# Two cross-attention stages: which PSUM bank holds what, and in which order TensorE, ScalarE and VectorE use them

## The chip, the cores and the metric
One core of a Trainium2 chip runs the whole program. The metric is device time in microseconds: the median of three executions.

## The reference, cut to what matters
Six residual stages on x (2 sequences of 256 tokens, width 256), each on the layer-normed x. The first and the fourth are cross-attention to a context of 4096 rows of width 256:

```python
q = (x @ Wq); k = (context @ Wk); v = (context @ Wv)      # stage 1: 8 heads of 64; stage 4: 16 heads of 16, with biases
scores = einsum("bhnd,bhmd->bhnm", q, k) * scale
out = einsum("bhnm,bhmd->bhnd", softmax(scores), v)
x = x + out @ Wo + bo
```

The others are local and latent attention, a dense mixture of experts, a linear recurrence, and a mixture over sorted chunks. They are not touched.

## The kernel before, in words
Each cross-attention runs over four units (a sequence and half of the heads), and a unit over eight chunks of 512 context rows: 32 chunks. A chunk of the context is loaded into `c_in` (SyncE), transposed on TensorE (`turn`, two banks of four 128x128 transposes, line 935), and split into a high part `c_hi` (ScalarE, `context_high`, line 641) and a low part `c_lo` (VectorE, `context_low`, line 1542), since matmuls take fp32r. From these come the keys (`keys`, in the first stage two tiles of six 512-column matmuls, in the fourth one, line 948) and values (`values`, two blocks of twelve 256-column matmuls each; in the fourth stage only for units 0 and 2). Keys are again split into a high part (lines 678, 679, 762) and a low part (`low_keys`, lines 1578, 1579, 1687).

Softmax needs the maximum over all keys before the first exponential. So for each chunk `maxima` multiplies high parts of keys and queries (lines 993 and 1148; two 512-column matmuls for each h, 8 matmuls a chunk in stage 1 and 16 in stage 4), and VectorE reduces each bank of 128x512 to one column (`reduce`, lines 1567 and 1676). Only when a unit's eight chunks are through does `shift_row` bring the negated maxima (DMA) into the row that the exact scores add. Scores, exponentials and mixtures therefore run LAG = 9 chunks behind: step t handles keys and values of chunk t, maxima of chunk t-1, and scores and mixtures of chunk g = t-9. Steps 1 to 8 have maxima only, steps 9 to 31 have all ("full steps"), the last ones scores and mixtures only. The program lists steps per engine by hand: every engine executes its instructions in the written order, with waits on semaphores between them.

PSUM has eight banks. Two pairs are `score[0]` and `score[1]` (1024 columns each), `bank[1]` gathers the mixture, and the other three are a `ring`: the uses of a step (denominators, maxima, keys, values, transposes) take the three in turn, and `freed0`/`freed1` say which earlier use's semaphore (`red`, `kl`, `v`, `cl`, `dc`) has to be waited for. In the fourth stage the order on TensorE in a full step is: score pair n and maxima pair n for n = 0 to 7, the first mixture after n = 5 (four heads, 32 matmul records of 256 columns, line 1161), keys, the second mixture, values, transposes of the next chunk. VectorE: all reductions, low part of keys, end of a unit (`finish`: reciprocal, product, bias), `context_low`, high queries (first step of a unit) and low queries (two in each of four steps). GpSimd copies the split keys into `st1` for the scores. Below, R, S and M are reductions, score pairs and maxima pairs.

## Time and profile before

| | us |
|---|---|
| median of 3 runs | 1932.55 (1932.42 to 1935.55) |
| the profiled execution | 1927.47 |
| its span, first to last instruction | 1925.5 |
| TensorE busy | 1664.0 |
| VectorE busy | 1117.2 |
| ScalarE busy | 793.3 |
| GpSimd busy | 499.8 |

A row of the timeline merges equal instructions that follow each other: start, length, engine, line, operation, output<-input, shapes, count, and in brackets the idle time before it with what ended it. PE is TensorE, PEld its weight loads, DVE VectorE, ACT ScalarE, POOL GpSimd. PEclk is the granted TensorE clock as a share of 2.4 GHz. Ends of matmuls are modelled, so starts are the safer reading.

### The profile page before, as it was taken

The page shows a single profiled execution, that of the slowest core. Times are in us where ns is not written, and L with a number is a line of the kernel's source. Part 1 is how long each engine was busy: PE and PEld are TensorE (multiplying, and loading weights), DVE is VectorE, ACT ScalarE, POOL GpSimd, SP SyncE. Part 2 cuts the span into 40 slices and gives each one's busy share as a digit, 9 for nine tenths or more (in the row PEclk, how much of TensorE's full clock was granted, in tenths as well). Part 3 has the DMA queues.
Part 4 walks back from the last instruction along what each step waited for, and adds up shares of the span by engine and source line. Part 5 has one row for each costly group of instructions (what it writes and reads, how often), then busy time and mean ns, then how long its engine had stood idle before and what let it go on. Part 6 is the DMA issues. An engine that isn't in the chain of part 4 may idle for free. (4 is left out here: it accounts for less than half of the span.)

```text
span 1925.5 us, 26912 instructions
## 1 busy us (share of the span) xinstructions
PE 1664.0 (86%) x10311; PEld 1208.0 (63%) x10311; DVE 1117.2 (58%) x1880; ACT 793.3 (41%) x1084; POOL 499.8 (26%) x630
## 2 busy tenths in 40 slices
PE   5889999999999668779997888999999899885289
PEld 3667777777777467568886555555566555342278
DVE  4766666666653465356654777776756777106651
ACT  3435554554544132224442111555556455661110
POOL 0003433433469000000000200443433434640000
PEclk9989999999999877679998777899999999997589
DMA  2112221222222100022230110111001010000243
GB/s 77 44 44 67 66 61 50 67 67 58 53 60 52 33 1 1 23 88 87 87 98 11 33 32 27 31 34 34 23 23 34 23 34 12 2 1 22 88 156 117
DMA packets 75443, 92.35 MB, mean 48 GB/s; under 512 B 7442, under 2 KB 62276, under 8 KB 75332
## 3 DMA queue, kind: packets, MB, share of 16 engines
q1 hardware_dynamic: 75140, 90.79, 15.8%
q8 instruction: 73, 1.20, 0.3%
q14 instruction: 38, 0.31, 0.1%
q10 hardware_dynamic: 192, 0.05, 0.0%
HBM read 73.47 MB, written 0.52 MB: 38 GB/s over the span
## 5 line engine op out<-in xcount | busy, mean ns | idle before, releaser
L571 POOL CAST st<-ef 32x512 fp32r<-32x512 f32 x384 | 233.0, 607 | 397.9 <-PE score L1136 354.4
L1676 DVE TENSOR_REDUCE mx<-bank 128x1 f32<-128x512 f32 x512 | 311.8, 679 | 42.2 <-PE bank L1148 41.6
L757 ACT ACTIVATE P<-score 128x1024 f32<-128x1024 f32 x256 | 255.9, 1025 | 129.1 <-PE score L1136 128.8
L1148 PE MATMUL bank<-ef,qm 128*128 128x512 f32 x512 | 234.4, 505 | 41.3 <-DVE mx L1676 21.4
L948 PE MATMUL bank<-c_hi,w_split 128*128 128x512 f32 x640 | 233.1, 425 | 23.7 <-DVE c_lo L1542 8.4
L1148 PEld LDWEIGHTS bank<-ef,qm 128*128 128x128 f32 x512 | 105.9, 207 | 154.9 <-DVE mx L1676 107.4
L1136 PE MATMUL score<-qs,st 97*128 97x512 f32 x512 | 173.3, 426 | 12.9 <-ACT P L757 8.7
L948 PEld LDWEIGHTS bank<-c_hi,w_split 128*128 128x128 f32 x640 | 128.7, 201 | 78.1 <-issue 39.8
L1567 DVE TENSOR_REDUCE mx<-bank 128x1 f32<-128x512 f32 x256 | 162.3, 682 | 22.1 <-PE bank L993 13.6
L536 POOL TENSOR_TENSOR sum<-sum,P 128x512 f32<-128x512 f32 x84 | 111.2, 1324 | 210.0 <-ACT P L673 210.0
L673 ACT ACTIVATE P<-score 128x1024 f32<-128x1024 f32 x128 | 129.9, 1024 | 78.5 <-PE score L982 76.0
L1542 DVE TENSOR_TENSOR c_lo<-bank,c_hi 128x512 fp32r<-128x512 f32 x128 | 82.4, 685 | 128.8 <-ACT c_hi L641 128.7
L948 PE MATMUL bank<-w_split,c_hi 128*128 128x256 f32 x768 | 144.6, 288 | 0.0
L981 PE MATMUL score<-qh,k 128*128 128x256 f32 x512 | 132.2, 291 | 2.0 <-ACT P L673 2.0
L948 PE MATMUL bank<-c_lo,w_split 128*128 128x512 f32 x320 | 132.0, 413 | 0.0
L948 PEld LDWEIGHTS bank<-w_split,c_hi 128*128 128x128 f32 x768 | 120.9, 192 | 14.8 <-issue 12.2
L982 PE MATMUL score<-ql,w 65*128 65x256 f32 x512 | 128.9, 285 | 0.0
L1136 PEld LDWEIGHTS score<-qs,st 97*128 97x128 f32 x512 | 92.8, 196 | 55.5 <-issue 23.2
L1161 PE MATMUL bank<-P,v 128*17 128x256 f32 x2048 | 126.0, 384 | 1.2
L1005 PE MATMUL bank<-P,v 128*64 128x256 f32 x1024 | 123.4, 385 | 0.4 <-ACT P L673 0.4
L993 PE MATMUL bank<-k,qh 128*128 128x512 f32 x256 | 98.8, 443 | 20.4 <-DVE c_lo L1542 13.7
L538 POOL TENSOR_TENSOR sum<-sum,P 128x512 f32<-128x512 f32 x84 | 110.3, 1313 | 6.6
(315 smaller groups left out, 2646.0 us busy)
## 6 DMA issues: line engine op xcount, KB each, us to landing
c_in<-in_ctx SPq DMA_DIRECT2D x64, 512.0 KB, 4.0
w<-k SPq DMA_DIRECT2D x128, 128.0 KB, 2.2
arena<-in_L_ffn_w SPq DMA_DIRECT2D x16, 1024.0 KB, 5.2
arena<-in_L_ffn_W SPq DMA_DIRECT2D x16, 1024.0 KB, 5.4
x<-in_x SPq DMA_DIRECT2D x1, 512.0 KB, 3.7
raw<-in_L_xattn_Wk SPq DMA_DIRECT2D x1, 512.0 KB, 6.4
raw<-in_L_xattn_Wv SPq DMA_DIRECT2D x1, 512.0 KB, 7.3
raw<-in_L_xattn_Wq SPq DMA_DIRECT2D x1, 512.0 KB, 8.1
```

The costliest lines, as they stand in the source:

```text
L571: pool.tensor_copy(st1[32 * block:32 * block + 32, k, :], ef1[rows, g % LAG, part, :].bitcast(F32)).then_inc(a[f"st{k}"], 16)
L673: act.activation(P[:, h, :], score[h % 2][:], ACT.Exp).then_inc(a["p"], 1)
L757: act.activation(P1[:, index % PRING, :], score[n % 2][:], ACT.Exp).then_inc(a["p"], 1)
L948: last = mm(dst, l, r, start=(n == 0), stop=(n == len(pairs) - 1))
L981: mm(o, k0[:, g % LAG, h, keys], qh0[:, u % 3, h, :], start=True, stop=False)
L982: last = mm(o, w0[0:65, h, keys], ql0[0:65, u % 2, h, :], start=False, stop=True)
L1005: last = mm(mix[64 * j:64 * j + 64, S * n:S * n + S], v0[:, g % LAG, k, 64 * h:64 * h + 64], P[:, h, S * k:S * k + S], start=False, stop=F ...
L1136: last = mm(score[n % 2][:, 512 * j:512 * j + 512], st1[0:97, pair, 128 * k:128 * k + 128], qs1[0:97, u % 2, 2 * pair:2 * pair + 2, :], st ...
L1148: mm(dst[:], qm1[:, h, 128 * q:128 * q + 128], ef1[:, g % LAG, 0, :], start=True, stop=True).then_inc(a["ms"], 1)
L1161: last = mm(mix[32 * j:32 * j + 17, S * quad:S * quad + S], v1[:, (NCH * (u // 2) + i) % VRING, k, h, :], P1[:, index % PRING, S * j:S * j ...
L1567: v.tensor_reduce(mx0[:, u % 2, i, n:n + 1], ring[(1 + n) % 3][:], AX.X, ALU.max).then_inc(a["red"], 1)
L1676: v.tensor_reduce(mx1[:, u % 2, i, n:n + 1], ring[n % 3][:], AX.X, ALU.max).then_inc(a["red"], 1)
```

## The change
The helpers `freed0`/`freed1` and the place numbers are replaced by named uses: `place_of` gives a use its bank, `freed` searches back for the last use of the same bank. First stage: places stay as they were. Fourth stage, steps 9 on: transposes, keys and both value blocks all use one bank, the maxima alternate between the other two; steps 0 to 8: keys one bank, values and transposes two. In both stages the maxima of chunks 0 to 7 go into `score[h % 2]`, two matmuls side by side, and one reduction of 128x2x512 (`reduce_early`) reads both. In steps 0 to 8 keys and values stand between maxima on TensorE. In full steps of the fourth stage a chunk is transposed in its own step, after n = 1 and n = 4; its `context_low` follows the reductions of h = 2 and 5; the last one or two maxima pairs (`ahead_of` says which) come after the keys, and the low part of keys comes before the last reductions. After the last maxima the second mixture moves into the next step.

```diff
@@ -176,45 +176,65 @@
         ring = (bank[0], bank[2], bank[3])
         mix = bank[1]
 
...
+
+        order0 = ["d", *(f"m{n}" for n in range(8)), "k0", "k1", "v0", "v1", "t0", "t1"]
+        place0 = {use: n % 3 for n, use in enumerate(order0)}
+
+
+        order1 = ["t0", "t1", *(f"m{n}" for n in range(16)), "k0", "v0", "v1"]
+        early1 = ["k0", "v0", "v1", "t0", "t1"]
...
+            if kind == "v":
+                return ("v", values1(t // NCH, t % NCH) + n + 1) if t // NCH % 2 == 0 else None
+            return ("kl", t + 1) if kind == "k" else ("cl", 2 * chunk + n + 1)
+
+        def uses_of(a, t):
+            return order0 if a is a0 else order1 if t >= LAG else early1
+
+        def place_of(a, t, use):
+
+            if a is a0:
+                return place0[use]
+            if use[0] == "m":
+                return 1 + int(use[1:]) % 2
+            return 0 if t >= LAG else {"k0": 0, "v0": 1, "v1": 2, "t0": 1, "t1": 2}[use]
+
+        def bank_of(a, t, use):
+            return ring[place_of(a, t, use)]
+
+        def freed(a, t, use):
+
+            place, done = place_of(a, t, use), done0 if a is a0 else done1
+            earlier = uses_of(a, t)[:uses_of(a, t).index(use)]
+            while t >= -1:
+                for other in reversed(earlier):
+                    if place_of(a, t, other) == place and done(t, other):
+                        return done(t, other)
+                t -= 1
+                earlier = uses_of(a, t)
+            return None
 
         program = ctx.enter_context(nc.Block())
 
...
@@ -792,24 +812,33 @@
                 for t in range(STEPS):
                     g = t - LAG
                     u, i = divmod(t, NCH)
-                    if g > 0 and g % NCH == 0:
+                    if g < 0:
+                        keys(t)
+                        if u % 2 == 0:
+                            values(u, i, 0)
+                            values(u, i, 1)
+                        if t + 1 < LAG:
+                            for f in range(2):
+                                context_high(a, c_hi, t, t + 1, f)
+                        if t == NCH:
+                            shift_row(0)
+                        continue
+                    if g and g % NCH == 0:
                         sums(g // NCH - 1)
-                    if g >= 0:
-                        for n in range(8):
-                            weights(g, n)
+                    for n in range(8):
+                        weights(g, n)
+                        if n in (1, 4) and t < CHUNKS:
+                            context_high(a, c_hi, t, t, n // 4)
                     if t < CHUNKS:
                         keys(t)
-                    if g >= 0 and g % NCH == NCH - 1:
+                    if g % NCH == NCH - 1:
                         mixed(g // NCH)
                     if t < CHUNKS and u % 2 == 0:
                         values(u, i, 0)
-                    if i == 0 and 0 < t <= CHUNKS:
+                    if i == 0 and t <= CHUNKS:
                         shift_row(u - 1)
                     if t < CHUNKS and u % 2 == 0:
                         values(u, i, 1)
-                    if t + 1 < CHUNKS:
-                        for f in range(2):
-                            context_high(a, c_hi, 19 + f, t + 1, f)
                 sums(UNITS - 1)
 
 
...
@@ -988,9 +1017,12 @@
                         pe.wait_ge(a["qh"], a.n("qh", 8 * u + 2 * h + 2))
                     if h % 2 == 0:
                         pe.wait_ge(a["kl"], a.n("kl", 2 * g + h // 2 + 1))
+                    early = g + 1 < LAG
+                    if early and 4 * g + h >= 2:
+                        pe.wait_ge(a["red"], a.n("red", 8 * g + 2 * h - 2))
                     for q in range(2):
-                        dst = place_free(a, freed0, g + 1, 1 + 2 * h + q)
-                        mm(dst[:], qh0[:, u % 3, h, 128 * q:128 * q + 128], k0[:, g % LAG, h, :], start=True, stop=True).then_inc(a["ms"], 1)
+                        dst = score[h % 2][:, 512 * q:512 * q + 512] if early else place_free(a, g + 1, f"m{2 * h + q}")[:]
+                        mm(dst, qh0[:, u % 3, h, 128 * q:128 * q + 128], k0[:, g % LAG, h, :], start=True, stop=True).then_inc(a["ms"], 1)
 
                 def mixture(g, n):
                     u, i = divmod(g, NCH)
...
@@ -1054,14 +1087,18 @@
                             scores(g, h)
                         if 1 <= t <= CHUNKS:
                             maxima(t - 1, h)
+                        if g < 0 and h:
+                            if h < 3:
+                                keys(t, h - 1)
+                            if h == 3 and t == NCH:
+                                shift_row(0)
                     if g >= 0:
                         mixture(g, 0)
-                    if t < CHUNKS:
-                        keys(t, 0)
-                        keys(t, 1)
-                    if t % NCH == 0 and 0 < t <= CHUNKS:
-                        shift_row(t // NCH - 1)
-                    if g >= 0:
+                        if t < CHUNKS:
+                            keys(t, 0)
+                            keys(t, 1)
+                        if t % NCH == 0 and t <= CHUNKS:
+                            shift_row(t // NCH - 1)
                         mixture(g, 1)
                     if t < CHUNKS:
                         if t == 0:
...
@@ -1199,35 +1239,54 @@
                     if t == 1:
                         queries()
                         output_weights()
-                    if g > 0 and g % NCH == 0:
+                        pe.wait_ge(set1["q"], 2)
+                        pe.wait_ge(set1["wop"], 2)
+                    if g < 0:
+                        for h in range(8):
+                            if t:
+                                maxima(t - 1, h)
+                            if h == 1:
+                                keys(t)
+                            if h in (3, 5) and u % 2 == 0:
+                                values(t, h // 2 - 1)
+                        if t + 1 < LAG:
+                            turn(a, t, t + 1, 0)
+                            turn(a, t, t + 1, 1)
+                        if t == NCH:
+                            shift_row(0)
+                        continue
+                    if g == 0:
+                        pe.wait_ge(set1["st"], 1)
+                        pe.wait_ge(set1["ones"], 1)
+                    if g and g % NCH == 0:
                         sums(g // NCH - 1)
+                    ahead_of = 8 if i == 0 else 7 if u % 2 else 6
                     for n in range(8):
-                        if t == LAG and n == 0:
-                            pe.wait_ge(set1["q"], 2)
-                            pe.wait_ge(set1["wop"], 2)
-                            pe.wait_ge(set1["st"], 1)
-                            pe.wait_ge(set1["ones"], 1)
-                        if g >= 0:
-                            if n == 1 and g and g % NCH == 0:
-                                pe.wait_ge(a["dc"], a.n("dc", g // NCH))
-                            scores(g, n)
-                        if 1 <= t <= CHUNKS:
+                        if n == 1 and g and g % NCH == 0:
+                            pe.wait_ge(a["dc"], a.n("dc", g // NCH))
+                        scores(g, n)
+                        if t <= CHUNKS and n < ahead_of:
                             maxima(t - 1, n)
-                        if g >= 0 and n == 5:
+                        if n in (1, 4) and t < CHUNKS:
+                            turn(a, t, t, n // 4)
+                        if n == 1 and t > CHUNKS + 1 and g % NCH:
+                            mixture(g - 1, 1)
+                        if n == 5:
                             mixture(g, 0)
                     if t < CHUNKS:
                         keys(t)
-                    if g >= 0:
+                    if t <= CHUNKS and ahead_of < 8:
+                        maxima(t - 1, ahead_of)
+                    if t <= CHUNKS or g % NCH == NCH - 1:
                         mixture(g, 1)
+                    if t <= CHUNKS and ahead_of < 7:
+                        maxima(t - 1, 7)
                     if t < CHUNKS and u % 2 == 0:
                         values(t, 0)
-                    if i == 0 and 0 < t <= CHUNKS:
+                    if i == 0 and t <= CHUNKS:
                         shift_row(u - 1)
                     if t < CHUNKS and u % 2 == 0:
                         values(t, 1)
-                    if t + 1 < CHUNKS:
-                        turn(a, freed1, 19, t + 1, 0)
-                        turn(a, freed1, 19, t + 1, 1)
                 pe.wait_ge(set1["bias"], 16 * 21)
                 output(set1, a, oT1, wout1, sums)
...
@@ -1536,10 +1595,15 @@
                 v.tensor_copy(xnT[:, 1, :], bank[1][:]).then_inc(ln["xT"], 1)
                 dve.wait_ge(ln["xT"], ln.n("xT", 2))
 
-            def context_low(a, hi, lo, place, g, f):
+            def context_low(a, hi, lo, t, g, f):
 
                 dve.wait_ge(a["ch"], a.n("ch", 2 * g + f + 1))
-                v.tensor_tensor(lo[:, f, :], ring[(place + f) % 3][:], hi[:, f, :].bitcast(F32), ALU.subtract).then_inc(a["cl"], 1)
+                v.tensor_tensor(lo[:, f, :], bank_of(a, t, f"t{f}")[:], hi[:, f, :].bitcast(F32), ALU.subtract).then_inc(a["cl"], 1)
+
+            def reduce_early(a, mx, per_chunk, g, h):
+
+                dve.wait_ge(a["ms"], a.n("ms", per_chunk * g + 2 * h + 2))
+                v.tensor_reduce(mx[:, 0, g, 2 * h:2 * h + 2], score[h % 2][:].rearrange("p (q k) -> p q k", q=2), AX.X, ALU.max).then_inc(a["red"], 2)
...
@@ -1615,12 +1679,16 @@
                         for n in range(4):
                             dve.wait_ge(set0["qp"], n + 1)
                             v.tensor_scalar(qT[:, n, :], score[n // 2][:, 512 * (n % 2):512 * (n % 2) + 512], 64 ** -0.5, None, ALU.mult).then_inc(set0["q"], 1)
-                    if 1 <= t <= CHUNKS:
-                        for h in range(HPU0):
+                    for h in range(HPU0):
+                        if LAG <= t <= CHUNKS:
                             reduce(t - 1, h)
+                        if 1 <= t < LAG:
+                            reduce_early(a, mx0, 8, t - 1, h)
+                        if t < LAG and h in (1, 2):
+                            low_keys(t, h - 1)
                     if t % NCH == 0 and 0 < t <= CHUNKS:
                         maximum(t // NCH - 1)
-                    if t < CHUNKS:
+                    if LAG <= t < CHUNKS:
                         low_keys(t, 0)
                         low_keys(t, 1)
                     if g > 0 and g % NCH == 0:
...
@@ -1711,18 +1779,28 @@
                         high_queries(0)
                         dve.wait_ge(set1["wop"], 1)
                         v.tensor_copy(wout1[:], score[1][:].rearrange("p (k n) -> p k n", k=4)).then_inc(set1["wop"], 1)
-                    if 1 <= t <= CHUNKS:
-                        for h in range(HPU1):
+                    ahead_of = 8 if i == 0 else 7 if u % 2 else 6
+                    for h in range(HPU1):
+                        if LAG <= t < CHUNKS and h == min(ahead_of + 1, 7):
+                            if ahead_of < 8:
+                                low_keys(t)
+                        if LAG <= t <= CHUNKS:
                             reduce(t - 1, h)
+                        if 1 <= t < LAG:
+                            reduce_early(a, mx1, 16, t - 1, h)
+                        if t < LAG and h == 1:
+                            low_keys(t)
+                        if LAG <= t < CHUNKS and h in (2, 5):
+                            context_low(a, c_hi, c_lo, t, t, h // 4)
                     if i == 0 and 0 < t <= CHUNKS:
                         maximum(u - 1)
-                    if t < CHUNKS:
+                    if LAG <= t < CHUNKS and ahead_of == 8:
                         low_keys(t)
                     if g > 0 and g % NCH == 0:
                         finish(g // NCH - 1)
-                    if t + 1 < CHUNKS:
+                    if t + 1 < LAG:
                         for f in range(2):
-                            context_low(a, c_hi, c_lo, 19, t + 1, f)
+                            context_low(a, c_hi, c_lo, t, t + 1, f)
                     if i == 0 and 0 < t < CHUNKS:
                         high_queries(u)
                     if i in (1, 2, 3, 4) and t < CHUNKS:
```

`turn`, `context_high`, `context_low`, `keys` and `values` now ask `bank_of` for their bank. On TensorE, step 1 of the fourth stage waits for `q` and `wop` (the queries' and output weights' reads of the score buffers) before its first maxima, and step 1 of the first for `q`.

## Rows read from the trace of the kernel before

**Rows 1.** The page, busy us, share and instructions of each engine.
```profile
PE 1664.0 (86%) x10311; PEld 1208.0 (63%) x10311; DVE 1117.2 (58%) x1880; ACT 793.3 (41%) x1084; POOL 499.8 (26%) x630
```

**Rows 2.** Stretches: length, busy us of PE, PEld, DVE, ACT, POOL, PEclk, DMA share, GB/s.
```profile
41.40:146.60 105.20, 92.05 (x425) 65.64 (x426) 72.27 (x117) 42.77 (x80) 0.00 (x0) 0.92 0.14 41
1067.60:1204.70 137.10, 121.11 (x412) 74.92 (x413) 99.18 (x170) 24.27 (x41) 8.74 (x15) 0.75 0.10 31
1203.00:1324.00 121.00, 113.44 (x774) 68.05 (x775) 87.37 (x147) 68.20 (x78) 55.88 (x92) 0.95 0.10 31
1324.00:1484.20 160.20, 150.20 (x1082) 96.59 (x1081) 104.94 (x174) 88.19 (x108) 63.49 (x104) 1.00 0.09 27
1484.20:1624.60 140.40, 127.84 (x882) 74.25 (x881) 105.16 (x173) 78.80 (x90) 63.51 (x104) 0.98 0.09 27
```

**Rows 3.** Timeline, DVE, fourth-stage opening step: start, length, instructions, idle before.
```profile
1100.78 1.29 DVE L1542 TENSOR_TENSOR c_lo<-bank,c_hi 128x512 fp32r<-128x512 f32 x2 [2.51 <-ACT c_hi L641]
1102.10 0.87 DVE L1668 SCALAR_TENSOR_TENSOR qs<-qT,mask_16th,qm 32x256 fp32r<-32x256 f32 x2
1103.00 9.66 DVE L1676 TENSOR_REDUCE mx<-bank 128x1 f32<-128x512 f32 x16
1114.81 0.75 DVE L1687 SCALAR_TENSOR_TENSOR ef<-bank,bias,ef 128x512 fp32r<-128x512 f32 x1 [2.15 <-ACT ef L762]
```

**Rows 4.** Timeline, PE, the same step.
```profile
1112.59 1.00 PE L948 MATMUL bank<-c_hi,w_split 128*128 128x512 f32 x2
1113.43 0.39 PE L948 MATMUL bank<-c_lo,w_split 128*128 128x512 f32 x1
...
1113.89 0.40 PE L948 MATMUL bank<-w_split,c_hi 128*128 128x256 f32 x2
...
1116.75 1.04 PE L935 MATMUL bank<-ident,c_in 128*128 128x128 f32 x8
```

**Rows 5.** Timeline, DVE, first-stage opening step.
```profile
54.47 4.86 DVE L1567 TENSOR_REDUCE mx<-bank 128x1 f32<-128x512 f32 x8
61.17 0.68 DVE L1578 TENSOR_TENSOR k<-bank,k 64x512 fp32r<-64x512 f32 x1 [1.84 <-ACT k L679]
...
65.46 1.29 DVE L1542 TENSOR_TENSOR c_lo<-bank,c_hi 128x512 fp32r<-128x512 f32 x2 [1.48 <-ACT c_hi L641]
```

**Rows 6.** Timeline, DVE, full step of the fourth stage.
```profile
1257.20 1.29 DVE L1542 TENSOR_TENSOR c_lo<-bank,c_hi 128x512 fp32r<-128x512 f32 x2 [1.59 <-ACT c_hi L641]
...
1259.43 7.27 DVE L1676 TENSOR_REDUCE mx<-bank 128x1 f32<-128x512 f32 x12
1268.24 2.48 DVE L1676 TENSOR_REDUCE mx<-bank 128x1 f32<-128x512 f32 x4 [1.55 <-PE bank L1148]
1272.06 0.75 DVE L1687 SCALAR_TENSOR_TENSOR ef<-bank,bias,ef 128x512 fp32r<-128x512 f32 x1 [1.34 <-ACT ef L762]
```

**Rows 7.** Timeline, PE, the same step.
```profile
1256.73 0.71 PE L1136 MATMUL score<-qs,st 97*128 97x512 f32 x2
...
1260.17 0.50 PE L1148 MATMUL bank<-ef,qm 128*128 128x512 f32 x1 [1.03 <-DVE mx L1676]
...
1265.38 1.92 PE L1161 MATMUL bank<-P,v 128*17 128x256 f32 x32
1267.23 0.73 PE L1136 MATMUL score<-qs,st 97*128 97x512 f32 x2
...
1273.08 1.09 PE L935 MATMUL bank<-ident,c_in 128*128 128x128 f32 x8
```

**Rows 8.** Groups by line: count, busy us, mean ns of one, idle before.
```profile
L767 ACT ACTIVATE v<-bank 128x512 f32<-128x512 f32 x32 | 19.2, 599 | 40.4 <-PE bank L948 40.4
...
L1790 DVE TENSOR_REDUCE arena<-arena 128x16 f32<-128x4096 f32 x2 | 8.8, 4407 | 0.0
```

**Rows 9.** Timeline, DVE, end of a unit in the fourth stage.
```profile
1518.06 3.34 DVE L1555 RECIPROCAL den<-den 128x512 f32<-128x512 f32 x1
...
1523.34 1.27 DVE L1542 TENSOR_TENSOR c_lo<-bank,c_hi 128x512 fp32r<-128x512 f32 x2
```

113 lines of the change are left out of this document (50 added, 63 removed).

## The prediction
> **What bounds the kernel now.** I read the page first: TensorE is busy 86% of the span and VectorE 58% [rows 1], which says only that no engine is full in both cross-attention stages, the two that the diff touches. So I cut these stages by steps, with the busy times of each stretch [rows 2]. The first stage's opening (steps 1 to 8, which have maxima but no scores) takes 105.2 us, 13.2 a step; VectorE is busy 72.3 of it. The fourth stage's opening, from its first reduction to that of step 9, takes 137.1 us, 17.1 a step, VectorE 99.2, granted clock 0.75. The fourth stage's full steps take 121.0 us for steps 9 to 15 (17.3 each), 160.2 for 16 to 23 (20.0, with values), 140.4 for 24 to 31 (17.6). No engine fills them: TensorE's busy time there is modelled and includes waiting for weights, so I counted issue intervals instead, from the timeline.
>
> In an opening step of the fourth stage VectorE reduces 16 banks in 9.66 us, 0.60 each, then sits idle 2.15 us for the keys to be projected and copied, and 2.51 us for the transposes of the next chunk and their copy [rows 3]. TensorE behind it issues one 512-column matmul per reduction, then keys, values and transposes in one block [rows 4]. The ring makes these take turns: maxima of step t+1 can't start before the transposes' bank is freed by c_lo. In the first stage it is the same with 8 reductions (4.86 us) and idle times of 1.84 and 1.48 us [rows 5]. In a full step of the fourth stage the idle times are 1.55 (TensorE is in the first mixture), 1.34 (keys) and, before c_lo, 1.59 [rows 3, 6]; TensorE for its part waits 1.03 us and more for reductions [rows 7]. So the step is a chain that alternates between two engines, and what shortens it is overlap.
>
> **Unit prices.** TensorE at full clock: a 512-column matmul 0.235 us (1113.43 to 1113.89 has two), at half clock 0.42 (1112.59 to 1113.43); 24 value matmuls 2.86; a chunk's transposes 0.87 [rows 4, 7]; a mixture 1.85 (1265.38 to 1267.23) [rows 7]. Per full step: 8 score pairs and 8 maxima pairs 32 x 0.235 = 7.5, keys 1.45, two mixtures 3.7, transposes 0.87: 13.5, with values 16.4. VectorE: reduction 0.60 back to back, c_lo 2 x 0.61, ef 0.67, low queries 0.87 in half the steps [rows 3].
>
> **Part 1: one 1024-wide reduction in place of two 512-wide, in the openings.** 32 pairs in the first, 64 in the fourth stage. The trace has no such reduction from two banks. Bounds: nothing saved (2 x 0.60 = 1.20), and a width-only price: the 4096-wide reduction takes 4407 ns [rows 8], 1.04 ns an element and some 140 fixed; the 512-wide one takes 0.68 of which 0.08 overlaps with the next, so a 1024-wide one is 1.21, and 1.13 back to back. I take 1.13. The Trainium skill, Perfetto Trace Analysis, section Optimizing Scalar/DVE Operations, gives VectorE about 125 ns of access overhead per instruction on PSUM and says that grouping helps a saturated engine; by it the pairs would save 96 x 0.125 = 12 us of VectorE, where the trace's 0.60 per 512 leaves 0.07 and so 6.7 us. The trace decides.
>
> **Part 2: fourth stage's opening.** Maxima leave the ring for two double-wide score buffers, keys and values get a bank each, and their matmuls stand between pairs of maxima. VectorE then has 8 x 1.13 + 0.67 + 1.22 + 0.87 = 11.8 us. Chain beside it: c_lo ends, keys 1.45 + 0.15, ef copy 0.69, and ef's low part is due 2.4 us later, just as low queries and two reductions (3.1) end: covered. A value block (1.43) ahead of the sixth pair makes that pair some 0.35 late; transposes run beside the last two reductions (2.3 us against 0.87 + two copies of 0.6: covered). So 12.3 a step with low queries (1 to 4), 11.5 without (5 to 7). Step 8 has the maximum, the shift row through a DMA and the high queries after its reductions: 14.0. Sum 4 x 12.3 + 3 x 11.5 + 14.0 = 97.7, plus 0.6 for the new wait in step 1 (nothing is queued behind it but maxima, which needed the high queries anyway). Against 137.1: -38.8 at full clock. Before, the clock was at 1.2 GHz for part of each step, in and after the long row of single maxima [rows 2, 4]; if it stays there all the time, TensorE needs for an opening step 22 x 0.42 (16 maxima, 6 keys) + 5.7 (values doubled) + 1.7 = 16.7, and the gain falls to 5 (7 x 16.7 + 14.0 + 0.6 = 131.5). The row of maxima is now broken up by dense blocks, but they are still there; I charge 0.8 a step: **-33** (bounds -5 and -39).
>
> **Part 3: first stage's opening.** VectorE: 4 x 1.13 + 4 x 0.70 (key low parts, 0.68 and the step to the next [rows 5]) + 1.22 + 0.4 (half the fourth stage's low queries) = 8.9. Chain: c_lo to keys 1.55, two key copies 1.2 (0.60 for 512 columns on ScalarE [rows 8]), low parts 1.4 (after R0, R1: at 2.95), third reduction to 5.5, second low parts to 6.9, transposes 0.45, copy 0.6, c_lo 1.2: 9.6 a step. TensorE in it has 2 x 4 maxima, 12 key, 24 value matmuls and transposes: 8.5, under the chain. Step 1, where ScalarE makes eight query copies first, 10.8. Step 8 now has the shift row ahead of values and transposes on TensorE; it waits for the last reduction and the maximum, and values, transposes, c_hi and c_lo are queued behind it: last reduction at 8.05 after c_lo, maximum and shift row 0.5, values 2.86, transposes 0.87, and 1.5 by which the first maxima run ahead of c_lo: 13.8. Sum 10.8 + 6 x 9.6 + 13.8 = 82.2 against 105.2. **-23** (bounds -10, where half of the idle time stays, and -27, VectorE's own work). First-stage full steps keep places and order: 0.
>
> **Part 4: full steps of the fourth stage.** Two banks for maxima in place of three. A bank's round is reduction 0.68, 0.05 to the wait's end, matmul 0.50, 0.04: 1.27 per pair, against 1.20 for VectorE alone. Step: score and maxima pairs 0 to 5 with the transposes among them take 8.7: the first reduction starts at 1.0; five rounds of 1.27, 0.6 for c_lo and 0.45 where transposes hold up the third pair put the sixth pair's at 8.4, and the mixture follows its matmuls (it was 8.65 without transposes: 1256.73 to 1265.38 [rows 7]); then mixture 1.85, S6 M6 S7 1.4, keys 1.45, M7 0.47, mixture 1.85: 15.7; the keys' wait (the low part of keys stands before the last reduction) lies under the mixture. So the transposes' 0.87 and the waits for c_lo at the start of a step go: 17.3 to 15.7, and 15.85 where low queries delay the first reduction. With values the two value blocks share one bank: the second waits for the copy, 0.15 + 0.60 + 0.05 = 0.8 [rows 8]; its cover (the shift row) is there in one step of eight. 15.7 + 2.86 + 0.8 = 19.4 against 20.0. The unit's end on VectorE (reciprocal to last add, 5.2 us: 1518.06 to 1523.34 [rows 9]) stands between the last reduction and the next step's first; it is not hidden now (5.0 of it shows; 2.1 in the steps with values).
> Steps 9 to 15: 4 x 15.85 + 3 x 15.7 = 110.5, and 2 for a clock of 0.95 as before: -8.5. Steps 16 to 23: 8 x 19.4 + 2.1 + 0.3 = 157.6: -2.6. Steps 24 to 31: 4 x 15.7 + 4 x 15.85 + 5.0 + 1.6 (high queries) + 0.3 = 133.1: -7.3. **-18** (bounds: +5, every pair at 1.35 and one more wait of 0.5 in each of the 23 steps; -60, TensorE's pure work of 13.5 and 16.4). The tail (mixture one step later) is paced by exponentials and stays: 0.
>
> **Sum.** -33 - 23 - 18 = -74. The profiled execution took 1927.5 (span 1925.5 and 2 around it), so it would be 1853; the median of the runs is 5.1 above that execution: 1932.6 - 74 = **1858**.
>
> **Rivals.**
> (a) The openings gain, the full steps don't: five users of one bank and the 1.27 round eat the overlap. For it: VectorE's and TensorE's shares both come near the step length, so small delays add. Against: 3 us of idle a step on each side [rows 6, 7]. 1932.6 - 56 = 1877.
> (b) The fourth stage's opening stays at 1.2 GHz, as 0.75 in [rows 2] suggests: -5 in place of -33: 1886.
> (c) The wide reduction isn't what it seems: reading two banks costs 1.36 (0.68 twice). Then 96 x 0.23 = 22 us come back on the engine that paces both openings: 1880.
> (d) Slower. In full steps TensorE now stops for one of two banks at each pair; if the granted clock, 0.95 to 1.00 there now, falls, each of the 38 wide matmuls costs 0.19 more and mixtures more likewise, 7 to 8 us a step at full effect. From 3.2 us a step (74 over 23 steps), some 45% of the work at 1.2 GHz, the change loses; at 60% it is 1932.6 + 25 = 1958. Against: the steps' front has more matmuls in the same 8.7 us than before, and ran at 1.00 [rows 7]. The Trainium skill, TensorE: Matmul & The Clock Gate, section A second HAM failure mode: psum-queue depth-cycling, describes just this: TensorE idling briefly at each cycle through its PSUM banks, and the clock swinging. By that rule the opening at 0.75 agrees, the full steps don't.
> (e) Better than forecast: full steps close in on TensorE's work by half and the openings run at full clock: 1932.6 - 105 = 1828.
>
> **Chances.** Forecast 0.55 (own range 1843 to 1872), (a) 0.16, (b) 0.10, (c) 0.06, (d) 0.04, (e) 0.07, and 0.02 for no change at all, gains and new waits cancelling. Range 1832 to 1890: it holds the forecast, (a), (b), (c) and part of (e). Faster by over 0.2% (about 4 us, what a measurement here can tell from no change) 0.94, within 0.2% 0.02, slower 0.04.
>
> **What would show it.** Opening steps of 12.3 and 11.5 us in the fourth and 9.6 in the first stage; reductions 128x1024 at 1.21 us, 1.13 apart; VectorE's idle before ef and c_lo gone there; granted clock above 0.85 in that opening. Full steps of 15.7 to 15.9, and 19.4 with a 0.8 us gap between the value blocks. First-stage full steps at 17.0 as before and tails unchanged. Wrong if the opening stays above 15 us a step, if full steps stay at 17.2, or if the clock of steps 9 to 31 falls below 0.9.

## The result, and the profile after

| | before | after |
|---|---|---|
| median, 4 runs each, taken together | 1934.05 | 1883.41 (1879.97 to 1889.59) |
| ratio, 95% interval | | 0.9738 (0.9707 to 0.9769) |
| the profiled execution, its span | 1927.47, 1925.5 | 1879.97, 1878.3 |

The kernel became 2.6% faster: 50.6 us by the medians, 47.5 between the profiled executions. Forecast were 74 and 1858; the time is inside the stated range, outside the forecast's own narrower range (1843 to 1872), and nearest to rival (a).

The page of the kernel after, engines [rows 1] and the new reduction (busy us, mean ns):

```profile
PE 1603.4 (85%) x10311; PEld 1193.4 (64%) x10311; DVE 1122.9 (60%) x1784; ACT 790.6 (42%) x1084; POOL 500.8 (27%) x630
...
L1606 DVE TENSOR_REDUCE mx<-score 128x2 f32<-128x1024 f32 x96 | 112.8, 1217 | 7.6 <-PE score L1188 5.2
```

Windows of the kernel after, cut at the same events as [rows 2], with the first stage's opening ahead of them; the first row shows the columns:

```profile
core 0: us, PE busy (x) PEld busy (x) DVE busy (x) ACT busy (x) POOL busy (x), PEclk, DMA share, GB/s
41.80:126.70 84.90, 73.87 (x425) 61.56 (x426) 71.43 (x85) 43.47 (x80) 0.00 (x0) 0.98 0.18 50
1049.80:1152.10 102.30, 81.66 (x403) 58.20 (x403) 93.76 (x104) 23.52 (x39) 7.41 (x13) 0.97 0.12 37
1151.40:1268.20 116.80, 109.19 (x776) 66.23 (x775) 89.17 (x141) 67.17 (x77) 55.77 (x92) 0.98 0.11 32
1268.20:1432.90 164.70, 150.92 (x1082) 99.29 (x1081) 108.32 (x173) 85.69 (x107) 63.88 (x105) 0.99 0.09 27
1432.90:1575.00 142.10, 127.34 (x890) 76.78 (x889) 109.36 (x173) 78.46 (x92) 63.35 (x104) 0.96 0.10 27
```

| stretch | before | after | difference | forecast |
|---|---|---|---|---|
| first stage, opening | 105.2 | 84.9 | -20.3 | -23 |
| first stage, full steps | 468.5 | 468.5 | 0 | 0 |
| up to the fourth stage's first reduction | 452.5 | 454.6 | +2.1 | in the 0.6 of Part 2 |
| fourth stage, opening, up to step 9's first reduction | 137.1 | 102.3 | -34.8 | -33 |
| steps 9 to 15, 16 to 23, 24 to 31 | 121.0, 160.2, 140.4 | 116.8, 164.7, 142.1 | -4.2, +4.5, +1.7 | -8.5, -2.6, -7.3 |
| from the scores of step 32 to the end | 301.5 | 303.8 | +2.3 | 0 |

(The windows cut full steps at their first maxima matmul. These sum to -48.7; what remains to the -47.2 of the spans is 0.4 ahead of the first opening, 1.0 between step 9's first maxima and first reduction, which both rows above count, and rounding.) So the two openings give 55 us and the full steps nothing: they win 4 in steps 9 to 15 and lose 6 after. The 2.3 of the last row is no more than that row varies: it takes 305.5 us in experiment 1, where the fourth stage's tail is the old one, and 302.0 in experiment 5, where it is the new one.

**The fourth stage's opening.** VectorE in one step, c_lo to c_lo, in the kernel after [rows 3 before]:

```profile
1061.80 1.28 DVE L1601 TENSOR_TENSOR c_lo<-bank,c_hi 128x512 fp32r<-128x512 f32 x2
...
1064.00 2.36 DVE L1606 TENSOR_REDUCE mx<-score 128x2 f32<-128x1024 f32 x2
1066.28 0.74 DVE L1755 SCALAR_TENSOR_TENSOR ef<-bank,bias,ef 128x512 fp32r<-128x512 f32 x1
1066.93 4.61 DVE L1606 TENSOR_REDUCE mx<-score 128x2 f32<-128x1024 f32 x4
1072.08 2.36 DVE L1606 TENSOR_REDUCE mx<-score 128x2 f32<-128x1024 f32 x2 [0.54 <-PE score L1188]
1074.35 1.28 DVE L1601 TENSOR_TENSOR c_lo<-bank,c_hi 128x512 fp32r<-128x512 f32 x2
```

The two idle times of [rows 3] are gone; 0.54 is left, where the second value block stands ahead of a maxima pair. The step is 12.55 us. Two reductions in a row take 2.36: 1217 ns each, 1.14 from start to start.

**A plain full step** (14 or 15: no values, no low queries, no unit's end). TensorE and then VectorE before, in step 14:

```profile
1291.12 0.71 PE L1136 MATMUL score<-qs,st 97*128 97x512 f32 x2
...
1298.74 1.92 PE L1161 MATMUL bank<-P,v 128*17 128x256 f32 x32
...
1306.44 1.09 PE L935 MATMUL bank<-ident,c_in 128*128 128x128 f32 x8
1307.28 0.71 PE L1136 MATMUL score<-qs,st 97*128 97x512 f32 x2
```

```profile
1292.80 7.25 DVE L1676 TENSOR_REDUCE mx<-bank 128x1 f32<-128x512 f32 x12
```

and after, in step 14:

```profile
1235.40 0.73 PE L1173 MATMUL score<-qs,st 97*128 97x512 f32 x2
...
1242.90 0.60 PE L964 MATMUL bank<-ident,c_in 128*128 128x128 f32 x4
...
1244.36 1.92 PE L1201 MATMUL bank<-P,v 128*17 128x256 f32 x32
...
1249.64 1.92 PE L1201 MATMUL bank<-P,v 128*17 128x256 f32 x32
1251.49 0.50 PE L1173 MATMUL score<-qs,st 97*128 97x512 f32 x1
```

```profile
1236.41 2.57 DVE L1744 TENSOR_REDUCE mx<-bank 128x1 f32<-128x512 f32 x4 [0.54 <-PE bank L1188]
1239.43 1.29 DVE L1744 TENSOR_REDUCE mx<-bank 128x1 f32<-128x512 f32 x2 [0.45 <-PE bank L1188]
...
1244.23 1.29 DVE L1744 TENSOR_REDUCE mx<-bank 128x1 f32<-128x512 f32 x2 [0.44 <-PE bank L1188]
```

16.16 us before, 16.09 after, from scores to scores. Behind the first mixture the step did become shorter, 8.54 to 7.13: no transposes at the end (0.84), no wait for the last reductions ahead of the keys. Its front grew by as much, 7.62 to 8.96. Before, VectorE reduced twelve banks without a stop (7.25, 0.60 each); with two banks and transposes in between it waits 0.54 before its first reduction, 0.45 before the third pair's and 0.44 before the sixth pair's.

### The profile page after: what moved, and what is told of

Read it like the earlier page. It is cut to its first block and busy times, and to the rows that moved or that the text cites. A ratio compares the mean times of both kernels' runs of the same rounds, so it can differ in the third digit from the quotient of the medians.

```text
span 1878.3 us, 26909 instructions
## 1 busy us (share of the span) xinstructions
PE 1603.4 (85%) x10311; PEld 1193.4 (64%) x10311; DVE 1122.9 (60%) x1784; ACT 790.6 (42%) x1084; POOL 500.8 (27%) x630
## 3 DMA queue, kind: packets, MB, share of 16 engines
q1 hardware_dynamic: 75140, 90.79, 16.3%
## 5 line engine op out<-in xcount | busy, mean ns | idle before, releaser
L1744 DVE TENSOR_REDUCE mx<-bank 128x1 f32<-128x512 f32 x384 | 246.9, 685 | 96.8 <-PE bank L1188 96.1
L777 ACT ACTIVATE P<-score 128x1024 f32<-128x1024 f32 x256 | 251.3, 1023 | 124.7 <-PE score L1173 124.6
L977 PE MATMUL bank<-c_hi,w_split 128*128 128x512 f32 x640 | 223.6, 407 | 26.1 <-DVE c_lo L1601 16.1
L1173 PE MATMUL score<-qs,st 97*128 97x512 f32 x512 | 174.1, 429 | 16.8 <-ACT P L777 11.5
L1188 PE MATMUL bank<-ef,qm 128*128 128x512 f32 x384 | 151.1, 445 | 30.1 <-DVE mx L1744 21.0
L977 PEld LDWEIGHTS bank<-c_hi,w_split 128*128 128x128 f32 x640 | 122.9, 192 | 73.6 <-issue 22.4
L693 ACT ACTIVATE P<-score 128x1024 f32<-128x1024 f32 x128 | 130.0, 1025 | 78.5 <-PE score L1011 76.1
L1188 PEld LDWEIGHTS bank<-ef,qm 128*128 128x128 f32 x384 | 73.1, 192 | 100.5 <-DVE mx L1744 80.5
L1631 DVE TENSOR_REDUCE mx<-bank 128x1 f32<-128x512 f32 x192 | 123.4, 685 | 20.4 <-PE bank L1025 12.2
L977 PEld LDWEIGHTS bank<-w_split,c_hi 128*128 128x128 f32 x768 | 122.5, 193 | 19.1 <-issue 8.8
L1173 PEld LDWEIGHTS score<-qs,st 97*128 97x128 f32 x512 | 88.4, 195 | 62.8 <-issue 42.2
L977 PE MATMUL bank<-c_lo,w_split 128*128 128x512 f32 x320 | 127.3, 398 | 0.0
L1606 DVE TENSOR_REDUCE mx<-score 128x2 f32<-128x1024 f32 x96 | 112.8, 1217 | 7.6 <-PE score L1188 5.2
```

The lines of the kernel that those rows point to most:

```text
L693: act.activation(P[:, h, :], score[h % 2][:], ACT.Exp).then_inc(a["p"], 1)
L777: act.activation(P1[:, index % PRING, :], score[n % 2][:], ACT.Exp).then_inc(a["p"], 1)
L977: last = mm(dst, l, r, start=(n == 0), stop=(n == len(pairs) - 1))
L1173: last = mm(score[n % 2][:, 512 * j:512 * j + 512], st1[0:97, pair, 128 * k:128 * k + 128], qs1[0:97, u % 2, 2 * pair:2 * pair + 2, :], st ...
L1188: mm(dst, qm1[:, h, 128 * q:128 * q + 128], ef1[:, g % LAG, 0, :], start=True, stop=True).then_inc(a["ms"], 1)
L1631: v.tensor_reduce(mx0[:, u % 2, i, n:n + 1], bank_of(a, g + 1, f"m{n}")[:], AX.X, ALU.max).then_inc(a["red"], 1)
```

## The experiments

Each is an edit of the kernel after, so helpers can stand a few lines lower. The diffs are cut to what matters; a line of dots marks a cut. "S9 to S32" is the time from the first scores of step 9 to those of step 32 (here S9 is a step, while S6 or M6 inside a step is its score or maxima pair). Times of single steps run from first scores to first scores, as listed from the traces; windows cut at the first maxima. S9 to S32 took 422.4 before, 424.1 after, 424.0 in a second execution of the kernel after, 424.1 and 424.3 in experiments 2 and 3, which leave these steps alone; 404 by the forecast. I read the verdicts from such stretches, not from totals, because code that no kernel touches varies: the stages between the two attention stages, in the kernel after and in the one with the unit end moved, with the same 2033 matmuls,

```profile
595.20:1043.60 448.40, 364.70 (x2033) 307.23 (x2031) 239.92 (x471) 138.75 (x225) 18.20 (x23) 0.85 0.15 47
```

```profile
596.90:1054.00 457.10, 372.42 (x2033) 312.02 (x2031) 239.93 (x471) 138.82 (x225) 18.14 (x23) 0.82 0.15 46
```

differ by 8.7 us with the granted clock of that execution, 0.85 and 0.82.

**1. Openings only.** Steps 9 to 31 of the fourth stage as before (three-bank ring, transposes of the next chunk last), openings as changed.

```diff
-            if use[0] == "m":
-                return 1 + int(use[1:]) % 2
-            return 0 if t >= LAG else {"k0": 0, "v0": 1, "v1": 2, "t0": 1, "t1": 2}[use]
+            if t >= LAG:
+                return order1.index(use) % 3
+            return {"k0": 0, "v0": 1, "v1": 2, "t0": 1, "t1": 2}[use]
...
```

> The changed kernel with the full steps (9 to 31) and the tail of the fourth stage put back: three banks in turn, transposes of the next chunk at the end of a step. Openings as changed. Theory A (the openings bring about 53 us, the new full steps nothing): fourth-stage openings at 12.7 us a step as in the changed kernel, full steps back at 17.2/16.2 and 20.2/19.1, and the whole within 4 us of the changed kernel, that is 51 to 55 us under the kernel before. Rival B (the full steps did gain their 18 us and something else, outside the steps, lost them): about 18 us slower than the changed kernel, 33 under the kernel before.

Measured: 1888.38 against 1929.97, ratio 0.979 (0.9773 to 0.9807). S9 to S32 422.5. The three stretches of full steps take 119.2, 162.5 and 140.9; the window of steps 16 to 23:

```profile
1272.20:1434.70 162.50, 152.48 (x1082) 100.46 (x1081) 105.55 (x173) 88.00 (x108) 63.51 (x104) 0.97 0.09 27
```

By this stretch theory A holds: the old full steps give 422.5 with the new openings and 422.4 without, so the openings carry the gain. By the totals it is less clean: 41.6 us under the kernel before, where A had 51 to 55 and B 33. The stretches leave no room for B's 18; experiments 2 and 3 came out as slow in the same set of runs. The equal sums hide unequal steps. Step 9 takes 16.7 for 18.8, but steps 18, 19 and 21 take 21.4, 21.0 and 21.1 for 20.8, 20.2 and 20.2, and each of the three has a piece of half clock, as step 10 has in both kernels:

```profile
1314.00:1323.00 9.00, 7.76 (x37) 5.31 (x41) 8.52 (x16) 5.24 (x6) 3.71 (x7) 0.81 0.17 58
```

Against this run the new order wins 2.4 in steps 9 to 15 (119.2 to 116.8; 1.4 of it in step 10) and loses 2.2 in 16 to 23 (162.5 to 164.7) and 1.2 behind (140.9 to 142.1).

**2. Narrow reductions.** Everything as changed, but two 512-wide reductions for each pair in the openings.

```diff
-                v.tensor_reduce(mx[:, 0, g, 2 * h:2 * h + 2], score[h % 2][:].rearrange(...), AX.X, ALU.max)
+                for q in range(2):
+                    v.tensor_reduce(mx[:, 0, g, 2 * h + q:...], score[h % 2][:, 512 * q:512 * q + 512], AX.X, ALU.max)
```

> The changed kernel, but in the openings each 128x2x512 reduction is two of 128x512 that wait for the same two matmuls. It takes the wide reduction away and leaves order and banks. Theory A (the gain of the openings is overlap, the wide reduction adds 0.07 us a pair): 96 x 0.07 = 7 us slower than the changed kernel, opening steps of the fourth stage 13.2 in place of 12.7, of the first 10.1 in place of 9.8. Rival C (the wide reduction is what pays): most of the 53 us gone, opening steps near 17 and 13. By the Trainium skill, Perfetto Trace Analysis, section Optimizing Scalar/DVE Operations (125 ns an instruction on PSUM): 12 us slower.

Measured: 1888.45, ratio 0.9797 (0.9775 to 0.9819). The first stage's opening grows by 0.7 (85.6), the fourth's by 2.8 (104.7 from the first maxima of step 1 to the first scores of step 9, against 101.9). Of these 2.8, 1.0 is in step 8 (17.3 for 16.3), which takes 17.1 in experiments 3 and 4 too, whose openings keep the wide reduction; the steps before it are 0.1 to 0.3 longer each. The same VectorE step of this kernel:

```profile
1067.51 2.48 DVE L1607 TENSOR_REDUCE mx<-score 128x1 f32<-128x512 f32 x4
...
1070.57 4.87 DVE L1607 TENSOR_REDUCE mx<-score 128x1 f32<-128x512 f32 x8
```

Four narrow ones take 2.48 where two wide ones take 2.36, 0.06 a pair. So the wide reduction is worth 3.5 of the 55 us at most, and the rest is overlap. What in it is the order on TensorE and what the two double-wide buffers, no run separates.

**3. Shift row later.** In step 8 of the first stage the shift row stands behind values and transposes on TensorE again, and likewise on ScalarE.

```diff
-                            if h == 3 and t == NCH:
-                                shift_row(0)
...
+                    if t == NCH:
+                        shift_row(0)
```

> The changed kernel with one move: in step 8 of the first stage the shift row comes after values and transposes, on TensorE and on ScalarE. Theory A (the 17.0 us of that step are TensorE's wait of 4.66 us for the maximum, with values, transposes and c_lo queued behind it, and half clock after it): the step falls to about 14 (the scores of step 9 wait for the maxima's DMA instead), 3 us faster than the changed kernel; the 4.66 us wait gone and TensorE's clock full in that step. Rival D (the DMA of the maxima sets the end of the step in either order): no change within 1 us.

Measured: 1889.61, ratio 0.9784 (0.9762 to 0.9806). Step 8 (between first maxima) takes 15.6 rather than 17.0, but step 9 17.9 rather than 17.3: 0.8 gained, which is rival D and not the 3 us of theory A. TensorE in that kernel at the first exact scores:

```profile
125.24 0.39 PE L1012 MATMUL score<-qh,k 128*128 128x256 f32 x1 [3.35 <-DMA ql<-shift]
```

The wait of 4.66 for the maximum has become one of 3.35 for the DMA that brings the row. The maximum, the transpose, its copy and the DMA are a chain of their own; values only fill the one hole or the other.

**4. Unit end split and moved.** Reciprocals, product and bias of a unit are spread over three steps; each part stands ahead of the last head's reductions (in steps with values, ahead of the last but one's), where VectorE waits for TensorE.

```diff
                     for h in range(HPU1):
+                        if g >= NCH and t < CHUNKS and i in (1, 2, 3) and h == (7 if u % 2 else 6):
+                            finish_part(g // NCH - 1, i - 1)
...
-                    if g > 0 and g % NCH == 0:
+                    if t > CHUNKS and g % NCH == 0:
                         finish(g // NCH - 1)
```

> The changed kernel with a unit's end on VectorE (reciprocal, product, bias, 5.2 us in one piece after the last reduction of steps 17 and 25) cut into three parts in steps 17 to 19 and 25 to 27, each ahead of a place where VectorE sits idle (before the reduction of h = 6 in steps with values, before h = 7 in those without). Theory A (unhidden unit ends are a loss of the new full steps): steps 17 and 18 together 43.2 to about 40.5, steps 25 and 26 together 40.0 to about 35.5, 6 us faster than the changed kernel. Rival (TensorE's waits there come from elsewhere, for example from the denominators' matmuls): the two pairs of steps stay within 1 us.

Measured: 1875.34, ratio 0.9707 (0.9681 to 0.9734). S9 to S32 414.4, 9.7 less, theory A with more than its 6. Step 18 goes from 23.1 to 19.9, step 26 from 23.7 to 17.0. In the kernel after, VectorE and TensorE at the start of step 26:

```profile
1468.66 3.34 DVE L1619 RECIPROCAL den<-den 128x512 f32<-128x512 f32 x1
...
1474.07 1.46 DVE L1736 SCALAR_TENSOR_TENSOR qs<-qT,mask_16th,qm 32x256 fp32r<-32x256 f32 x2
1475.56 1.29 DVE L1744 TENSOR_REDUCE mx<-bank 128x1 f32<-128x512 f32 x2
```

```profile
1476.31 1.39 PE L1188 MATMUL bank<-ef,qm 128*128 128x512 f32 x2 [6.36 <-DVE mx L1744]
```

With two banks TensorE gets one pair of maxima ahead of VectorE, so 6.90 us of other VectorE work stop it for 6.36. Behind the stop the granted clock was 0.56 for 7.2 us (1476.3 to 1483.5); in this experiment it was 1.00 over steps 24 to 31.

**5. Low queries moved.** They stand ahead of the seventh head's reductions (behind those of the sixth and `c_lo`), rather than ahead of the step's first reduction.

```diff
                     for h in range(HPU1):
+                        if h == 6 and i in (1, 2, 3, 4) and LAG <= t < CHUNKS:
+                            low_queries(u, 2 * i - 2)
+                            low_queries(u, 2 * i - 1)
...
-                    if i in (1, 2, 3, 4) and t < CHUNKS:
+                    if i in (1, 2, 3, 4) and t < LAG:
                         low_queries(u, 2 * i - 2)
                         low_queries(u, 2 * i - 1)
```

> The changed kernel with VectorE's low queries (0.9 us in steps 9 to 12, 17 to 20, 25 to 28) ahead of the reduction of h = 6, where VectorE is idle for 1.1 us, instead of at the end of a step, where the first reduction of the next step waits for them. Read from the stretches, since untouched stages differ by up to 9 us between executions. Theory A (VectorE is on the path from a step's first maxima to its mixture): steps 9 to 12 and 25 to 28 fall from 16.8 to about 16.3, steps with values stay, the stretch from the first scores of step 9 to those of step 32 falls from 424.1 to about 420. Rival (TensorE's matmuls pace the steps whatever VectorE does): no step changes by 0.2.

Measured, in one run: 1870.1, S9 to S32 415.6, 8.5 less where 4 were expected. Steps 10 to 13 and 27 to 29 go from 16.8 (17.0 in step 10) to 16.1, which is 4.9; the rest is mostly in steps 18 (23.1 to 21.6) and 26 (23.7 to 22.1), where low queries and unit end were in one queue. In that kernel low queries (0.89) run where VectorE had waited 1.10 for the seventh pair of maxima; 0.18 of the wait is left:

```profile
1212.16 1.29 DVE L1744 TENSOR_REDUCE mx<-bank 128x1 f32<-128x512 f32 x2 [0.18 <-PE bank L1188]
```

**6. Second value block in another bank.**

```diff
+            if use == "v1" and t >= LAG:
+                return 1
             return 0 if t >= LAG else {"k0": 0, "v0": 1, "v1": 2, "t0": 1, "t1": 2}[use]
```

> The changed kernel with the second value block of full steps in one of the two maxima banks (free there, since the last reductions lie before it) instead of the bank that the first block fills. Theory A (TensorE's stop of 0.7 to 0.85 us for the first block's copy is paid in full): the stop goes, the next step's first maxima come 0.3 later, so steps 17 to 23 fall from 20.0 to 19.5 and the stretch from 424.1 to about 420. Rival (the step is set by VectorE, the stop is free): 20.0 stays.

Measured, in one run: 1881.53, S9 to S32 422.0, 2.1 less. In the kernel after TensorE stops between the value blocks; here it doesn't, but the step's first maxima now wait for the copy:

```profile
1370.99 0.51 PE L977 MATMUL bank<-w_split,c_hi 128*128 128x256 f32 x2 [0.69 <-ACT v L787]
```

```profile
1353.98 0.70 PE L1190 MATMUL bank<-ef,qm 128*128 128x512 f32 x2 [0.31 <-ACT v L789]
```

From the last matmul of one block to the first of the other it was 0.97 us (0.12 where nothing waits): 0.85 lost. Now the first maxima are 0.94 behind the first scores rather than 0.47. So 0.47 of the 0.85 goes there, and steps 17 and 19 to 23 fall by 0.4 to 1.0 (19 to 23 from 20.0 to 19.6), as theory A had it. But step 18, with the unit's end in it, grows from 23.1 to 24.0, and step 24 from 19.5 to 20.0.

**7. Both transposes around the first mixture** (and c_lo behind the sixth head), so that they don't hold up maxima pairs.

```diff
-                        if n in (1, 4) and t < CHUNKS:
-                            turn(a, t, t, n // 4)
+                        if n == 5 and t < CHUNKS:
+                            turn(a, t, t, 0)
...
                         if n == 5:
                             mixture(g, 0)
+                        if n == 5 and t < CHUNKS:
+                            turn(a, t, t, 1)
```

> The changed kernel with the two groups of transposes of a full step no longer after n = 1 and n = 4, among the maxima, but one right before and one right after the first mixture; both low parts of the context follow the reduction of h = 5. Theory A (each group of transposes among the maxima costs VectorE 0.45 us, since with two banks there is no maximum in store): the front of a step, from its first scores to its first mixture, falls from 9.6 to 8.7 in steps without values, and the step from 16.8 to about 16.2; with values the keys then wait 0.5 for the low part, 20.0 to about 19.7; stretch 424.1 to about 414. Rival (the two-bank round of 1.28 us paces the front, transposes lie in its gaps): front unchanged, and the step 0.3 to 0.5 longer by the later low part.

Measured, in one run: 1887.73, S9 to S32 429.7, 5.6 more where 10 less were expected: my theory fell. TensorE of step 14 in that kernel, from the first mixture on:

```profile
1244.47 1.92 PE L1202 MATMUL bank<-P,v 128*17 128x256 f32 x32
1246.32 0.66 PE L965 MATMUL bank<-ident,c_in 128*128 128x128 f32 x4
1246.73 0.71 PE L1174 MATMUL score<-qs,st 97*128 97x512 f32 x2
```

The first mixture starts 8.39 us into the step rather than 8.96, as meant. But 0.41 comes back for the transposes behind it, and 0.27 for the keys, whose c_lo ends too late (scores to keys 0.74 rather than 0.47). That makes step 14 16.3 for 16.1; steps with low queries even win 0.1. Most of the loss, 4.6 of 5.6, is in steps 17 to 23, with values: there the keys of step 20 start 1.75 behind the seventh scores rather than 1.03, waiting for the late c_lo, and the step takes 20.5 for 20.0:

```profile
1368.49 0.47 PE L978 MATMUL bank<-c_hi,w_split 128*128 128x512 f32 x1 [0.57 <-DVE c_lo L1604]
```

Where transposes stand in the front, they lie in a time in which VectorE is the slower one; behind the mixture nothing covers them. Without them maxima pairs of step 14 start 1.27 to 1.32 apart (3.16, 4.43, 5.75 and 7.03 us into the step), which is the round of two banks by itself.

**8. Experiments 4, 5, 6 and 7 together** (low queries between the two c_lo).

> The changed kernel with all four: unit ends in three parts, second value block in a maxima bank, transposes around the first mixture, low queries between the two low parts of the context. Theory A (the losses are separate and add): 9.7 (measured for the unit ends alone) + 4 + 4 + 8 = 25 us off the stretch of 424.1: about 399; 25 us faster than the changed kernel, ratio to the kernel before about 0.961. Rival (they hide one another, since each only moves the wait to the other engine): less than 15.

Measured: 1880.95, ratio 0.9723 (0.9698 to 0.9749), S9 to S32 413.0, 11.0 less where 25 were expected: the rival, less than 15. It holds 7, and it is 8.2 longer than experiment 10 below, which has the other three edits (with the low queries in another place, so not all of the 8.2 need be the transposes).

**9. Unit end and low queries** (4 and 5 together), and **10. the value bank with them** (4, 5 and 6), and the kernel after once more, timed together. (The expectation of 9 puts the low queries between the seventh and the eighth head; the edit has them where experiment 5 has them, ahead of the seventh.)

> The changed kernel with two edits together: the low query words of the next unit are written between the seventh and the eighth head of the steps that write them (not ahead of the first), and the end of a unit (reciprocals, product, bias) is split over three steps and put behind the reductions of the last heads. Alone they took 9.7 (unit end) and 8.5 us (low queries) out of the 424.1 us from the scores of step 9 to those of step 32. A (Part 4 lost its gain to two pieces of work on VectorE that stand ahead of what TensorE waits for, each by itself): they add up but for the share of step 18 and step 26, where both were at work: 406 to 409, so a total near 1866. B (both shorten one and the same wait, so only the longer counts): 414 to 415, a total near 1872.

> As the kernel before it in this call, and the second half of a step's values in bank 1 rather than bank 0. Alone that edit made the twelve steps with values 19.5 us rather than 20.0 but the sum of the full steps only 2.1 us shorter, since step 18 grew. A: with the unit end out of the way the value bank gives its 0.4 to 0.5 in each of the 12 steps, 4 to 6 us less than the kernel without it: S9 to S32 401 to 404, a total near 1862. B (the wait of the second values is replaced by one of the maxima for bank 1): no difference from the kernel without it, within 2 us.

> The changed kernel once more, beside the other two: 1880 to 1886 by every theory; what counts is its distance to them, 14 to 20 us by A of the first, 8 to 11 by B.

| | median, 6 runs | ratio to before | S9 to S32 |
|---|---|---|---|
| 9: unit end, low queries | 1869.2 | 0.967 (0.9644 to 0.9697) | 407.9 |
| 10: and the value bank | 1867.25 | 0.9661 (0.9636 to 0.9685) | 404.8 |
| the kernel after | 1885.14 | 0.9756 (0.9729 to 0.9783) | 424.0 |

In kernel 10 steps 16 to 23 take 158.0; the windows of steps 9 to 15 and of 24 to 31:

```profile
1153.40:1267.30 113.90, 109.27 (x776) 66.14 (x775) 87.92 (x141) 67.17 (x77) 55.56 (x92) 0.98 0.12 33
...
1425.30:1557.80 132.50, 125.47 (x890) 74.84 (x891) 107.64 (x174) 77.76 (x91) 63.31 (x104) 1.00 0.10 29
```

The two pieces add up (16.1 of 9.7 + 8.5; the rest is step 18 and 26, where both saw the same wait): theory A of 9. The value bank takes the steps with values from 19.9 to 19.5 and S9 to S32 down by 3.1, a little under A (4 to 6) and over B (2). A counted twelve steps with values; the full steps have eight, 16 to 23, and 8 times 0.4 is 3.2. Steps without values take 16.1 throughout, and the clock of steps 24 to 31 is 1.00, not 0.96. Kernel 10 is 17.9 us under the changed one beside it in the same runs.

**11. The old full steps with the same pieces moved.** New openings, full steps of before (as in 1), low queries ahead of the seventh head's reductions, the unit's end in three parts behind the low part of keys.

```diff
                     for h in range(HPU1):
+                        if h == 6 and i in (1, 2, 3, 4) and LAG <= t < CHUNKS:
+                            low_queries(u, 2 * i - 2)
+                            low_queries(u, 2 * i - 1)
...
                     if LAG <= t < CHUNKS:
                         low_keys(t)
+                    if g >= NCH and t < CHUNKS and i in (1, 2, 3):
+                        finish_part(g // NCH - 1, i - 1)
```

> The new openings with the full steps of the kernel before (as in the first experiment: ring of three banks, the next chunk's transposes last), and the same two pieces of VectorE work moved as in the ninth: low queries ahead of the seventh head's reductions, the unit's end in three parts, here behind the low part of keys. The question is what the new order of the full steps is worth by itself. Read again from the trace of the kernel before, the full steps differ by what VectorE does beside: steps 14 and 15, which have no low queries, took 16.2 us there, 10 to 13 and 27 to 29 with low queries 17.2 and more, steps 22 and 23 (values, no low queries) 19.1, those with low queries 20.2; in the changed kernel 16.1, 16.8, 19.9 and 20.1. Theory A (the new order is worth 0.1 us in a step without values and loses 0.8 in one with values; the mean of 17.3 that the forecast cut down was low queries and unit ends, not transposes): the old order with both pieces moved has 16.2 and 19.1 throughout, S9 to S32 422.5 - 22 = 400 to 404, so as short as the best kernel so far (404.8) or shorter, total 1860 to 1867. Theory B (two banks and transposes in the own step are worth what the forecast said, over 1 us a step, and were hidden by the two pieces): the old order stays at 17 us in steps without values, S9 to S32 410 to 415, total above 1872.

Measured: 1865.49 (1860.14 to 1868.18), ratio 0.965 (0.9627 to 0.9673), S9 to S32 401.2. Its windows of steps 9 to 15, 16 to 23 and 24 to 31:

```profile
1153.10:1266.80 113.70, 110.70 (x775) 64.78 (x774) 84.82 (x140) 68.03 (x77) 55.82 (x92) 0.99 0.09 29
1266.80:1422.30 155.50, 150.09 (x1082) 96.56 (x1081) 104.29 (x175) 88.17 (x108) 63.58 (x104) 1.00 0.09 28
1422.30:1554.30 132.00, 126.50 (x882) 72.34 (x881) 104.70 (x174) 78.92 (x90) 63.62 (x104) 1.00 0.10 29
```

Steps 10 to 15 and 27 to 30 take 16.2 us, steps 18 to 23, with values, 19.1. That is theory A. Against kernel 9, which has the same two pieces moved and no other edit, the old order is 6.7 us shorter over the full steps (401.2 for 407.9); against kernel 10, 3.6 (steps with values 19.1 rather than 19.5). The ranges of the totals of 10 and 11 overlap. Both beat the kernel before, and the changed one by 1%; this is the shortest of all that ran. All that was edited between experiment 1 (422.5) and this one is where two pieces of VectorE work stand. Not all of the 21.3 is time that they took on VectorE: experiment 1 has the pieces of half clock in steps 10, 18, 19 and 21 and one behind the unit's end in step 26, and here the clock stays at full speed from step 10 to step 31. Those four steps had low queries ahead of their reductions and TensorE stopped behind them (1.57 us in step 10, 1.03 in step 18), but other such steps kept their clock; why some lost it is open.

## Why the prediction was right in part and wrong in part

**Part 1, right, and small.** 1.217 us for the wide reduction where 1.21 was worked out from two widths, 1.14 from start to start (1.13). I summed 96 x 0.07 = 6.7 us; experiment 2 gives 3.5 at most. Each pair saves 0.06. In the first stage's opening only 0.06 to 0.08 of it arrives in each of steps 2 to 7, for four pairs: there VectorE waits for copies and c_hi, so it isn't the pace. In the fourth stage's the idle time before the last two pairs falls from 0.54 to 0.33 and takes up a part. The Trainium skill, Perfetto Trace Analysis, section Optimizing Scalar/DVE Operations, has about 125 ns per instruction on PSUM; the trace shows 0.06 per instruction saved, and by the page's figure the openings would have lost 12 us in experiment 2, not 3.5.

**Part 2, right.** Steps of 12.6 (12.3 forecast), 11.8 (11.5), and -34.8 (between -33 and the ideal -38.8). The granted clock went from 0.75 to 0.97 there, as the charge for half clock supposed it mostly would: the 16 single maxima, each waiting for a bank, no longer stand in a row. It is 0.94 with narrow reductions (experiment 2) and 0.93 with wide ones in experiment 4, so order and banks do it and not the wide form; rival (b) is out. Two terms were small by some us: step 8 took 16.3 against 14.0, and the new wait in step 1 1.4 against 0.6.

VectorE at the fourth stage's first reduction in the kernel after:

```profile
1049.79 2.36 DVE L1606 TENSOR_REDUCE mx<-score 128x2 f32<-128x1024 f32 x2 [1.41 <-PE score L1188]
```

The maxima write into buffers that the copy of `wout` reads first, so they wait for its end (TensorE 4.90 us for `wout`); before they used the ring and ran beside it. (This wait lies ahead of the opening's window, in the +2.1 of the table.)

**Part 3, right but for step 8.** Steps of 9.8 (9.6 forecast, though the terms listed there add up to 9.15, from 6.9 behind the second low parts, 0.45, 0.6 and 1.2; that the number came so near is in part luck), step 1 9.2 to 10.8 between executions (10.8), step 8 16.8 to 17.1 against 13.8. TensorE and VectorE there, in the kernel after:

```profile
120.09 0.27 PE L1060 MATMUL score<-ident,mneg 128*8 128x128 f32 x1 [4.66 <-DVE mneg L1637]
...
121.07 0.63 PE L977 MATMUL bank<-w_split,c_hi 128*128 128x256 f32 x2
```

```profile
119.77 0.27 DVE L1637 TENSOR_REDUCE mneg<-mx 128x8 f32<-128x64 f32 x1
125.87 1.29 DVE L1601 TENSOR_TENSOR c_lo<-bank,c_hi 128x512 fp32r<-128x512 f32 x2 [5.84 <-ACT c_hi L661]
```

I had the order right (maximum, shift row, values, transposes, c_lo) and the wait, but priced what follows at full clock. After 4.66 us idle TensorE was granted 0.58 from 120.1 to 124.2, and the 24 value matmuls took 4.44 (120.12 to 124.56), not 2.86. To that the first scores of step 9 come, 1.35 ahead of its first maxima. Together 2.9 of the 3.2 missed. Experiment 3 shows that moving the row wins back 0.8 of it.

**Part 4, wrong: +2.0 measured against -18.** The step of the prediction that failed is "17.3 to 15.7". The means of [rows 2], 17.3 and 20.0, are means over unlike steps, and I took the 1.6 above my sum for transposes and waits for c_lo. Between first scores the kernel before took 16.2 us in steps 14 and 15, 17.2 in those with low queries (17.9 and 18.5 in steps 11 and 10, each with a piece of half clock); 19.1 in steps 22 and 23, 20.2 with low queries. So its plain steps were already where the new ones are, 16.2 against 16.1, and in steps with values the new ones are longer, 19.9 against 19.1. For the front I compared with 8.65 "without transposes" [rows 7], and that step had low queries (two of them ran ahead of its reductions, between the first and the second row of [rows 6], the line below); a plain one had 7.62. My own sum for the new front, 8.7, was then 1.1 worse than the old one (0.84 of it, the transposes, moved there from the end), and the profile said so.

```profile
1258.53 0.87 DVE L1668 SCALAR_TENSOR_TENSOR qs<-qT,mask_16th,qm 32x256 fp32r<-32x256 f32 x2
```

By size, forecast against measured (403.2 and 423.6 by windows; these shares are read off the step times, and only some were tried alone):

- *The plain step*, 16.1 for 15.7, in all 23: 9 us. The 1.27 round of two banks holds, but transposes stop VectorE twice in the front, 0.45 and 0.44, where I had one 0.45. So the sum that gave 8.4 for the sixth pair gives 8.83, where its first reduction starts (1244.23 against 1235.40), and the mixture starts at 8.96 and not 8.7. Behind it S6, M6, S7, M7 take 2.05 for 1.87.
- *Low queries*: 0.15 charged, 0.7 measured, and the first reduction starts 0.56 later (1.56 into the step rather than 1.01): some 4 us. (They cost the kernel before 1.0.)
- *Ends of units*: 5.0 and 2.1 charged, 6.9 and 3.1 measured: 3 us. (They cost the kernel before 4.5 and 0.6, steps 26 and 18 against 27 and 20; here two banks are worse than three.)
- *Values*: 0.8 charged for the wait, 0.85 measured. The mechanism was right, but it was a loss against 19.1 and not a gain against 20.0.
- *First steps of a unit*: step 16 takes 21.5, steps 24 and 25 35.8 together, step 9 17.3 (by its window), against charges of 0.3, 1.9 and nothing: 4 us.

That makes 20; the 2 that I had charged for the clock were not spent, and 0.2 more in each step with values takes their place. Low queries and unit ends were tried alone (5, 4) and add up (9); the value wait halves in another bank (10); the first terms are readings, which 11 bears out from the other side: with old steps and nothing in their way there are 16.2 and 19.1. What the first steps of a unit wait for was not tried.

So rival (a) came true; its -56 stands against 50.6 by the medians. Its reason, the 1.27 round and the bank with five users, is borne out in part: 0.4 us in a plain step and 0.85 in one with values are such losses. The larger part is the base: against old steps of 16.2 and 19.1 my own 15.7 and 19.4 are -0.5 and +0.3 a step, and not -1.6 and -0.6. The total came within 25 us because the openings, three quarters of the forecast, were right.

**Rivals.** (c): 1.217, not 1.36. (d): the granted clock of full steps was 0.96 to 0.99, as before. The Trainium skill, TensorE: Matmul & The Clock Gate, section A second HAM failure mode: psum-queue depth-cycling, speaks of idling at each cycle through banks; here waits of 0.2 to 0.7 for one of two banks left the clock up. It fell at longer stops, among them 4.66 in the first stage, 1.93 and 2.36 for maximum and shift row at the end of the fourth stage's step 8 (0.51 from 1148 to 1155), and 2.82 in step 18 and 6.36 in step 26, both at a unit's end. Rival (e) asked for -105; nothing here came near.

## What to carry to other kernels

Before a mean step is set against a sum of prices, list the steps one by one: what the mean has above the shortest is other work, and goes by moving that work and not by reordering the step (experiments 9 and 11: 16 to 21 us from two pieces moved, with either order, a part of the 21 by the clock; the new order won nothing before they were moved and cost 6.7 after). Put work that nobody waits for where its engine is idle, not ahead of the first thing that the other engine needs. A long misplaced piece cost more with two banks between the engines than with three (unit's end: 6.9 for 4.5 and 3.1 for 0.6), a short one did not (low queries: 0.7 for 1.0). What a kernel can gain by breaking an alternation of two engines is the idle time in it: VectorE was idle for 32.9 and 37.9 us of the two openings and is for 13.5 and 8.5 now, 49 of the 55 us.

## What the runs showed that I had not expected

Transposes moved out of a step's front made most steps longer (experiment 7): where VectorE was the slower of two engines in turns, they cost little, and behind the mixture the 0.41 of the second group was paid in full. And code that no kernel changed took 448.4 and 457.1 us in two executions, at granted clocks of 0.85 and 0.82, so totals of single executions can't tell effects under some 10 us here, while S9 to S32 of the same steps came out within 0.3 in four executions. The agreement can deceive too: the old full steps gave 422.4 and 422.5 with steps that differ by up to 2 us.
